# Weight groups of a quantised layer loaded ahead, page copies spread, and the inverses' row ahead of V, in a four-layer residual kernel

## The reference, cut to what matters

```python
x = x + L0(x)   # gated MLP (512 -> 1376 -> 512) with a LoRA adapter for each of the 8 sequences
x = x + L1(x)   # attention: 32 query heads, 8 key heads, 512 cached keys in pages + 128 new ones
x = x + L2(x)   # linear, weight quantised with a codebook and scale, plus a LoRA delta
x = x + L3(x)   # linear, one of 8 weights for each sequence

# L1, for each sequence and head
kc, vc = k_cache[block_table], v_cache[block_table]     # 16 pages of 32 keys
probs = softmax(where(valid, q @ k_all.T * SCALE, -1e30))
o = probs @ v_all ; y = o @ Wo.T

# L2: the weight is made once
wg = (weight + lora_delta).reshape(O, 4, 128) ; normalized = wg / exp(scale_log)
w_q = cb[searchsorted(thresholds, normalized)]          # passed through "+ normalized - normalized"
y = x @ (w_q * scale + lora_delta).T
```

## Time and profile before

| | us |
|---|---|
| median of three plain executions | 1434.79 |
| the profiled execution | 1438.17 |
| its span, first to last instruction | 1436.6 |
| TensorE busy (matmul) | 1378.2 |
| VectorE busy | 1020.5 |
| ScalarE busy | 980.1 |
| GpSimd busy | 748.7 |

### The profile page before, as it was taken

How to read it: one execution, slowest core, us unless ns; L and a number is a source line. 1 busy time by engine, 2 the same in 40 slices (tenths; PEclk the granted TensorE clock), 3 DMA queues, 4 the chain that set the end, 5 groups by cost and what they waited for, 6 DMA issues and landing times.

```text
span 1436.6 us, 26330 instructions
## 1 busy us (share of the span) xinstructions
PE 1378.2 (96%) x7812; PEld 1192.8 (83%) x7812; DVE 1020.5 (71%) x2111; ACT 980.1 (68%) x1986; POOL 748.7 (52%) x986
## 2 busy tenths in 40 slices
PE   7899897899999999999999999999999999999888
PEld 5788775688888888888888888888888888888766
DVE  4777666566777777777777777777777777777656
ACT  5666564467777687777776777777777777876643
POOL 5322222366666566656555665565566656655300
PEclk9999999999999999999999999999999999999989
DMA  8788778356332424333232334332323342322244
GB/s 196 229 263 274 229 182 270 99 135 174 96 89 60 104 59 113 71 98 77 72 104 60 90 73 115 63 89 60 103 60 95 75 111 60 89 59 60 40 173 147
DMA packets 256596, 165.80 MB, mean 115 GB/s; under 512 B 157398, under 2 KB 223575, under 8 KB 250951
## 3 DMA queue, kind: packets, MB, share of 16 engines
q1 hardware_dynamic: 250928, 144.51, 37.9%
q0 software_dynamic: 5376, 19.60, 4.8%
q10 hardware_dynamic: 150, 0.01, 0.0%
HBM read 158.66 MB, written 38.94 MB: 138 GB/s over the span
## 4 chain that ended last, share of the span: by engine, by line
PE 79%; DMA 5%; DVE 4%; ACT 3%; POOL 3%; issue 3%; SPq 2%; POOLq 0%; DVEq 0%; ACTq 0%
PE proj_ps L1366 16%; PE sc L1406 14%; PE o_ps L1444 13%; PE ring L1424 8%; PE sc L1161 5%; PE proj_ps L1460 4%; PE proj_ps L1463 4%; PE proj_ps L1471 4%; PE o_ps L1161 3%; DMA inv_row<-inv_dram 3%; PE proj_ps L1161 2%; DMA prep<-scale_dram 2%; PE ring L1483 2%; SPq L333 1%; POOL vl L631 1%
## 5 line engine op out<-in xcount | busy, mean ns | idle before, releaser
L1926 DVE TENSOR_TENSOR pTl<-ring,pTh 128x512 fp32r<-128x512 f32 x320 | 215.3, 690 | 144.7 <-ACT pTh L969 140.4
L958 ACT ACTIVATE p_sb<-p_sb,bias,rstd 128x640 f32<-128x640 f32 x256 | 236.0, 923 | 52.4 <-DVE bias L1909 52.4
L704 POOL TENSOR_TENSOR rstd<-var,half_neg 128x4 f32<-128x4 f32 x64 | 68.9, 1076 | 305.6 <-DVE var L1958 305.6
L1893 DVE CUSTOM_DVE_ANT_0 p_sb<-sc,mask 128x640 f32<-128x640 f32 x256 | 206.0, 823 | 23.7 <-PE sc L1406 17.9
L969 ACT ACTIVATE pTh<-ring 128x512 fp32r<-128x512 f32 x320 | 184.9, 601 | 27.7 <-PE ring L1424 26.4
L1424 PE MATMUL ring<-ident,p_sb 128*128 128x128 f32 x1280 | 181.4, 272 | 4.4 <-DVE pTl L1926 2.7
L1424 PEld LDWEIGHTS ring<-ident,p_sb 128*128 128x128 f32 x1280 | 152.8, 140 | 31.3 <-DVE pTl L1926 3.2
L1366 PE MATMUL proj_ps<-wh,xh 128*128 128x256 f32 (+1 forms) x484 | 168.2, 347 | 0.7 <-ACT q_sb L1005 0.7
L1406 PE MATMUL sc<-kTh,qTh 128*128 128x320 f32 x512 | 164.2, 321 | 2.9 <-DVE kTl L2000 2.9
L1366 PE MATMUL proj_ps<-wl,xh 128*128 128x256 f32 (+1 forms) x484 | 161.7, 334 | 0.0
L1005 ACT ACTIVATE q_sb<-proj_ps 128x512 f32<-128x512 f32 x64 | 38.3, 599 | 180.7 <-PE proj_ps L1366 172.2
(11 more groups left out here) (250 smaller groups left out, 3636.1 us busy)
## 6 DMA issues: line engine op xcount, KB each, us to landing
k_pages<-in_k_cache SPq DMA_DIRECT2D x128, 128.0 KB, 3.5
v_pages<-in_v_cache POOLq DMA_DIRECT2D x128, 128.0 KB, 3.7
k_raw<-k_pages SPq DMA_DIRECT2D x256, 64.0 KB, 2.6
v_raw<-v_pages SPq DMA_DIRECT2D x64, 256.0 KB, 3.0
rope<-rope_dram SPq DMA_DIRECT2D x64, 256.0 KB, 3.4
inv_row<-inv_dram SPq DMA_DIRECT2D x64, 256.0 KB, 3.9
stage<-in_Wqkv SPq DMA_DIRECT2D x32, 384.0 KB, 4.7
w_raw<-in_WguT SPq DMA_DIRECT2D x19, 512.0 KB, 4.8
```

The costliest lines, as they stand in the source:

```text
L704: pool.tensor_tensor(rstd[:, u.k % 2, 0:REP], var[:, u.k % 2, 0:REP], half_neg[:, 0:REP], ALU.pow).then_inc(S["q_pow"], 1)
L958: act_e.activation(p_sb[:, p_slot(u, h), :], p_sb[:, p_slot(u, h), :], ACT.Exp, bias=bias[:, h:h + 1], scale=rstd[:, u.k % 2, h:h + 1], ac ...
L1893: v.tensor_tensor_reduce(out=p_sb[:, p_slot(u, h), :].rearrange("p (s k) -> p s k", s=2), in0=score_ps[h % 2][:, :, 0:SPLIT], in1=mask[:, ...
L1926: v.tensor_tensor(pTl[:, c, :], ring[c % 2][:, :], pTh[:, c, :].bitcast(F32), ALU.subtract).then_inc(S["ptl"], 1)
```

## The change

Three parts. (1) Groups 1 to 3 of the quantised layer are loaded into `spare`, rows of the rotary table's tile, at q = 13, 16 and 20; `load_group` waits for the landing of the group before (group 1 also for the rotary table's write to DRAM, group 3 for group 2's stage 0) and no longer for its result. The results go to rows 2, 1, 0, 2 of `prep` (`made_row`); the wait for the store ahead of stage 0 goes, and group 3's result waits for the first store. The last group's stage 1 moves from right after `low_act(21)` to the step k = 2 of the last `down` steps, stage 2 from k = 3 to k = 4. (2) Key copies for each q come from a list, value copies are 4, then 3 (n = 11 to 15), then 7 (n = 16 to 21), then two for each block of W_down. Blocks of W_down 3 and 4 of the last steps are ordered ahead of the wait for `gate_up`; x is loaded at q = 18 and 21. (3) In a step of attention the row of inverses is ordered ahead of V, after two key copies where there are any. Some tiles of layers 1 and 2 are declared in another order.

```diff
+KEY_COPIES = [0] * 6 + [2, 2, 2, 3, 3] + [3] * 5 + [7] * 6
...
+        spare = rope_tab[:, :, :, :].rearrange("p k b d -> p (k b d)").rearrange("p (r n) -> p r n", n=HID)
...
+        def group_row(g, n):
+            return prep[:, n, :] if g == 0 else spare[:, 3 * (g % 2) + n, :]
+        def made_row(g):
+            return prep[:, (2, 1, 0, 2)[g], :]
...
                 else:
-                    sp.wait_ge(S["w2_ready"], g)
-                load(prep[:, 0, :], ins["W2T"][:, g, :], S["w2_in"])
...
+                    sp.wait_ge(S["w2_in"], 48 * g)
+                    if g == 1:
+                        sp.wait_ge(S["rope_in"], 16)
+                    if g == 3:
+                        sp.wait_ge(S["leaf_step"], 5)
+                load(group_row(g, 0), ins["W2T"][:, g, :], S["w2_in"])
...
-                sp.dma_start(w2_dram[:, g, :], prep[:, 4, :]).then_inc(S["put"], 16)
+                sp.dma_start(w2_dram[:, g, :], made_row(g)).then_inc(S["put"], 16)
...
-                if q == 13:
+                if q in (13, 16, 20):
+                    load_group({13: 1, 16: 2, 20: 3}[q])
+                if 19 <= q:
+                    load_wd(CH + q - 19)
+                if q == 18:
                     load(x_sb[:, 0:HALF, :], ins["x"][0:HALF].rearrange("b t n -> t b n"), x_in[0])
-                if q == 16:
+                if q == 21:
                     sp.wait_ge(S["xl_set"], 2 * C)
...
-                copy_keys(2 if q < FC else 5)
-                if q in (16, 19, 21):
+                if q in (16, 19):
                     store_group(q // 3 - 5)
-                    load_group(q // 3 - 4)
+                copy_keys(KEY_COPIES[q])
             copy_keys(5)
...
-            for n in range(FC):
-                if n >= 3:
-                    load_wd(CH + n)
-                    copy_keys(2)
-                if n == 5:
-                    store_group(3)
-                if n == 2:
+            store_group(2)
+            for n in range(3, FC):
+                load_wd(CH + n)
+                copy_keys(2)
+                if n == 4:
                     sp.wait_ge(S["gate_up"], 4 * FC)
                     for c in range(C):
                         load_wqkv(first, c)
                     load_k(first)
-                if n == 4:
+                if n == 5:
                     load_v(first)
...
+                if n == 6:
+                    store_group(3)
+                if n in (7, 9):
...
             def step(u):
                 put_inv(u + -2)
+                if u.k < B - 1:
+                    copy_keys(2)
+                spread_inv(u + -2)
                 if (u + -1).exists() and u.k > 1:
                     load_v(u + -1)
-                if 2 <= u.k < B - 1:
-                    copy_keys(2)
-                spread_inv(u + -2)
...
-                    copy_keys(6 if u.k < 2 else 4)
+                    copy_keys(4)
...
-                copy_values(4 if n < FC else 5)
-            pool.wait_ge(S["gate_up"], 4 * FC)
-            copy_values(18)
+                copy_values(4 if n < FC else 3 if n < 16 else 7)
+            for k in range(2, CH):
+                pool.wait_ge(S["wd_hi"], CH + k + 1)
+                copy_values(2)
...
-                if k == 5:
+                if k == 7:
                     act_e.wait_ge(S["put"], PUT_SCALES + 16 * C)
...
-                    if g:
-                        dve.wait_ge(S["put"], PUT_SCALES + 16 * g)
...
+                    if g == 3:
+                        dve.wait_ge(S["put"], PUT_SCALES + 16)
+                    v.tensor_tensor(made_row(g), tmp, delta, ALU.add).then_inc(S["w2_ready"], 1)
...
             low_act(2 * FC - 1)
-            weight2(*STAGES[2 * FC - 1])
...
                     low_t(1, 2)
-                if k == 3:
+                    weight2(*STAGES[2 * FC - 1])
+                if k == 4:
                     weight2(*STAGES[2 * FC])
```

More of the change, by code:

```diff
@@ L222, in cond_resid_kernel @@
         wl = l1_sb("wl", [P, C, QKV], F32R)
-        woh = l1_sb("woh", [P, REP, HID], F32R)
-        wol = l1_sb("wol", [P, REP, HID], F32R)
+        xh = l1_sb("xh", [P, B, C, T], F32R)
         rope = l1_sb("rope", [P, 2, 4, D])
@@ L227, in cond_resid_kernel @@
         v_raw = l1_sb("v_raw", [P, LC, D])
-        xh = l1_sb("xh", [P, B, C, T], F32R)
+        woh = l1_sb("woh", [P, REP, HID], F32R)
+        wol = l1_sb("wol", [P, REP, HID], F32R)
         xl = l1_sb("xl", [P, B, C, T], F32R)
@@ L269, in cond_resid_kernel @@
         w3_raw = l2_sb("w3_raw", [P, 2, C, HID])
+        w2_h = l2_sb("w2_h", [P, C, HID], F32R)
+        w2_l = l2_sb("w2_l", [P, C, HID], F32R)
         x2T_h = l2_sb("x2T_h", [P, 2, C * T], F32R)
@@ L274, in cond_resid_kernel @@
         w3_h = l2_sb("w3_h", [P, 2, C, HID], F32R)
-        w2_h = l2_sb("w2_h", [P, C, HID], F32R)
-        w2_l = l2_sb("w2_l", [P, C, HID], F32R)
         w3_l = l2_sb("w3_l", [P, 2, C, HID], F32R)
@@ L388, in load_group @@
                 else:
-                    sp.wait_ge(S["w2_ready"], g)
-                load(prep[:, 0, :], ins["W2T"][:, g, :], S["w2_in"])
-                load(prep[:, 1, :], scale_dram[0, g, :].partition_broadcast(P), S["w2_in"])
-                load(prep[:, 2, :], scale_dram[1, g, :].partition_broadcast(P), S["w2_in"])
+                    sp.wait_ge(S["w2_in"], 48 * g)
[4 more added lines that the diff above has]
+                load(group_row(g, 0), ins["W2T"][:, g, :], S["w2_in"])
+                load(group_row(g, 1), scale_dram[0, g, :].partition_broadcast(P), S["w2_in"])
+                load(group_row(g, 2), scale_dram[1, g, :].partition_broadcast(P), S["w2_in"])
             def store_group(g):
                 sp.wait_ge(S["w2_ready"], g + 1)
-                sp.dma_start(w2_dram[:, g, :], prep[:, 4, :]).then_inc(S["put"], 16)
+                sp.dma_start(w2_dram[:, g, :], made_row(g)).then_inc(S["put"], 16)
             load_x_chunk(0, 0)
@@ L423, in _ @@
                     load_wd(q - 8)
-                if q == 13:
+                if q in (13, 16, 20):
[3 more added lines that the diff above has]
+                if q == 18:
                     load(x_sb[:, 0:HALF, :], ins["x"][0:HALF].rearrange("b t n -> t b n"), x_in[0])
-                if q == 16:
+                if q == 21:
                     sp.wait_ge(S["xl_set"], 2 * C)
                     load(x_sb[:, HALF:, :], ins["x"][HALF:].rearrange("b t n -> t b n"), x_in[1])
-                if 19 <= q:
-                    load_wd(CH + q - 19)
-                copy_keys(2 if q < FC else 5)
-                if q in (16, 19, 21):
+                if q in (16, 19):
                     store_group(q // 3 - 5)
-                    load_group(q // 3 - 4)
+                copy_keys(KEY_COPIES[q])
             copy_keys(5)
@@ L490, in _ @@
                     load_rope(first)
-                if n in (6, 8):
-                    for h in (n - 6, n - 5):
+                if n == 6:
+                    store_group(3)
+                if n in (7, 9):
+                    for h in (n - 7, n - 6):
                         sp.wait_ge(S["wqkv_l"], h + 1)
@@ L1707, in weight2 @@
             def weight2(g, stage):
-                w, scale, norm, delta = (prep[:, n, :] for n in range(4))
+                w, scale, norm = (group_row(g, n) for n in range(3))
+                delta = prep[:, 3, :]
                 tmp = w
@@ L1731, in weight2 @@
                     then(v.tensor_tensor(tmp, tmp, scale, ALU.mult))
-                    v.tensor_tensor(leaf[0], tmp, delta, ALU.add).then_inc(S["w2_ready"], 1)
+                    if g == 3:
+                        dve.wait_ge(S["put"], PUT_SCALES + 16)
+                    v.tensor_tensor(made_row(g), tmp, delta, ALU.add).then_inc(S["w2_ready"], 1)
             def low_act(n):
```

## The result

The median of 11 plain executions is 1425.5 us (1420.3 to 1429.0), that of the kernel before on the same chip 1435.0 (11 executions, 1429.0 to 1437.4). The profiled executions stand at 1438.17 and 1428.24 us, 9.9 apart for a forecast of 19.6. The direction was right and the range (1411 to 1427) holds the median. But the sum was made from the profiled execution, and like with like, 1428.24 us, lies outside of it: some 40 to 50% of the gain is missing.

A forecast was written before the change was run, and what follows sets the result against it. TensorE was busy 96% of 1436.6 us, so gains had to come from its idle time or slow clock, some 58 us. Terms 10.3 + 0 + 2.5 + 6.8 = 19.6 took the profiled 1438.2 to 1418.6, range 1411 to 1427.

The forecast's parts named there:

- The groups' rows: Quantised layer, 104 to 230 us: earlier group loads remove TensorE's stalls and slow clock; 10.3 us, bounds 6 to 10.3.
- The copies up to block 21: SyncE's queue, q = 16 to 21: seven copies each stay within a margin of 1 to 5 us; cost 0, up to 3.5.
- Rival (c): SyncE's pacing: slower copies delay weight blocks, turning point 1.94 us spacing, 1447.6 us at 2.2; chance 0.04 full, 0.05 in part.
- The last `down` steps: 230 to 265 us: W_down blocks come less late, some 2.8 of 5.3 us idle stay; gain 2.5, bounds -1 to 5.3.
- the 2.6 of `lad_l`: The share of TensorE's 8.6 us of waits for `lad_l` forecast to go behind the end of `gate_up`; 2.6 us.
- a cost of 0: Price put on the new copy pacing, judged at weight block 21 on SyncE's queue; 0, upper bound 3.5 us.
- Stage 1 ahead of the fourth block: Last `down` steps: the last group's stage 1, 3.9 us, delays the fourth W_down block's split; a TensorE stall of 0.9 us.
- The loop's start: 265 to 300 us: a chain of latencies no edit touches; 0, with clock scatter worth 1.7 us either way.
- The row ahead of V: Attention loop: the row of inverses leaves sooner, ScalarE's waits shrink; 6.6 us plus 0.2, bounds 1 to 7.2 on the 6.6.
- (a): Weaker parts don't pay: last `down` steps give 0, the row of inverses 3; 1424.7 us; chance 0.30 together with (b).
- (b): Groups' stalls go but ScalarE takes over, so their part gives 6; 1422.9 us; chance 0.30 together with (a).
- (d): Gains don't add: TensorE's idle time moves to the loop's start; 1431 to 1436 us; chance 0.06.

The follow-up runs named there:

- e2: Changed kernel with V ordered ahead of the row of inverses again; 1428.0 us, ratio 0.9963.
- e11: Changed kernel with key and value copies paced as before the change, second run; 1419.4 us, ratio 0.9909.
- e8: Changed kernel with ten key copies for seven at each of q = 16 to 21; 1453.6 us in one execution.
- e10: Changed kernel run again with no edit; 1425.6 us, ratio 0.9956.
- e6: Changed kernel with the same transfers reordered on SyncE's queue, blocks of W_down at their earliest; 1416.9 us, ratio 0.9887.
- e9: Changed kernel with the order of e6 and the last group's stage 1 in three pieces; 1414.7 us, ratio 0.9885.
- e4: Changed kernel with the last group's stage 1 back right after the last `low_act`; 1425.7 us, ratio 0.9951.
- e12: Kernel before the change, run again with no edit for a second profile; 1433.7 us in one execution.
- e3: Changed kernel with key and value copies paced as before the change, first run; 1420.4 us, ratio 0.9909.
- e1: Kernel before with only the row of inverses ordered ahead of V; 1428.3 us, ratio 0.9967.
- e5: Changed kernel with the page copies beside the last W_down blocks moved into the loop's first steps; 1426.6 us, ratio 0.9942.

## Why the prediction was right or wrong

**The groups' rows: right.** -8.3 us up to G for -7.7. VectorE's wait for `prep<-scale_dram` is gone, so are the waits for `lad_l` and the half clock of the earlier trace rows; TensorE itself is what is late next, with 0.5 us idle in 108.4. G was forecast near 213 and came at 212.4. e2 to e11 repeat it (106.7 to 111.2 us for 116.3 to 116.7), e8 apart.

**The copies up to block 21: right.** Block 21 was forecast to be issued at 191 us and was at 192.6, with no wait of TensorE behind it; ScalarE waited 4.9 us for that block, which the slack covered. Rival (c) asked for slower orders, 1.94 us apart, and none came (1.25 to 1.39); e8 shows the same harm from more orders at the same spacing, and bounds the margin: block 21 ordered 22.4 us later brought 13.9 us more of idle time before G (14.4 for 0.5), so an estimate of it from these two runs is some 8 us, where the prediction had 1 to 5.

**The last `down` steps: the step that failed.** The prediction gave them -2.5 us, besides the 2.6 of `lad_l`; they got longer by 1.5, and so were 6.6 us over the forecast: 5.4 in idle time (8.5 for 3.1), 1.7 at half clock, and 0.5 of busy time the other way. Two terms of the step were wrong; both are about SyncE's queue. First, "a cost of 0" for the copies was taken at block 21 only. SyncE's lateness was inside the margin there and I let it drop, but the queue goes on: twelve copies (14.71 us) stand between block 21 and the next block of W_down, which goes out at 210.66 us, where the old pace has it at 204.10 (e11). With the order as it is, the new spread costs about 6 us, by e10 and e11; by e6 this lateness costs nothing that shows once the order is mended, so the two are not separate losses to be added. Second, the gain was put down to the two blocks ordered ahead of Wqkv and to the burst of value copies taken away. But block 6 still stands behind Wqkv's four loads and the keys' four and goes at 222.03, block 7 behind V, rotary rows and copies at 230.06. Where "blocks 7 and 8 still come 0 to 1.5 us late", the run has 2.0 us before block 7, 0.35 before block 8 and 3.1 before block 9, which had not been counted at all. e6 settles that it is the queue: the same transfers, reordered, give 38.9 us, which is the 39.2 that the prediction had for this stage, with the stage before it 1.7 us shorter as well. The bounds of this term, -1 to 5.3, did not hold it: it is a loss of 4.1 (1.5 more, and the 2.6 of `lad_l` used up). They took in neither the queue's lateness nor the clock; only with the up to 3.5 us that the prediction allowed for the copies at block 21 do they reach it. The sum's size was wrong in this term, and the kinds of wait were named.

**Stage 1 ahead of the fourth block.** Counted as a stall of 0.9 us from 222.6 on; it was 1.99, up to 223.93, and a half clock of 3.4 us stood behind it, 1.7 more. e9 shows what it is worth once the blocks come in time (37.6 us for the 38.9 of e6). e4 shows that it can't be had by putting the stage back.

**The loop's start: 0 forecast, +1.9.** Idle time is the same (10.0 for 9.7), the half clock 13.7 for 10.2 us, which is 1.75. Two profiles of one kernel differ by as much and more: 10.2 and 13.7 us (the first profile before and e12), 13.7 and 6.8 (e3 and e11), at 9.7 to 10.0 us idle. So this looks like scatter between executions, about the "1.7 us either way" of the prediction; no effect of the change is shown.

**The row ahead of V: right mechanism, size off by three.** 6.8 us forecast, 5.2 in the loop by the profiled pair, of which 3.3 are the event at units 21 to 23 that e12 doesn't have (loops of 1030.9 and 1027.6 us). The profiled pair owes a third of its whole gain of 9.9 us to that event, which is luck and not the change. The prediction had named this possibility, but left the 2.1 + 1.7 us in its sum. What stays is 1.9: by e12, 0.6 in units 1 to 5 (84.4 for 83.8) and some 1.2 at the heads' changes. A change takes 17.28 us after and 17.28 to 17.83 before, the event apart, so 0 to 0.5 us each for 0.35. ScalarE's 15.5 us of waits went to 0, and 6.1 us for `q_cos` came instead, the successor that the prediction named. The plain executions of e1 say 4.7 us (2.7 to 6.6); whether the rest over 1.9 is seldom-met waits like that of unit 22, which one profile can't show, stays open. Over 64 units the row goes 1.40 to 3.41 us after the inverses, half of them within 1.43; the prediction had 1.4 to 2.8.

**The median.** Against the medians the forecast was 1419.0 and the time 1425.5, 6.5 off, and 1.5 inside the range's edge. That it fell inside owes something to luck: the sum started from a profiled execution 3.4 us over the median; from the median the same 19.6 us give 1415.2, 10.3 off. e11, the same kernel with the old copies, has 1419.4, but not by the forecast's terms: its last `down` steps take 41.0 us for 39.2.

**The rivals.** (a), weaker parts that don't pay, named the right parts at 1424.7 us, of which the down steps were to give 0 and the row 3; they cost 4.1, and the row gave 5.2 in the profiled pair, of which 1.9 stay. Its 1424.7 is the nearest to the median, but it is made from the slower profiled execution too; against 1428.24 it is 3.5 short. (b) didn't come: 0.5 us for ScalarE. (d) did in part: what TensorE gained before G stayed, what it gained behind G went; its price (1431 to 1436) didn't come.

## What to carry to other kernels

When a queue of orders falls behind within its margin, carry the lateness on to the next consumer on that queue rather than dropping it where the first one is safe: here it was harmless at block 21 and, with the order of the queue as it was, cost some 6 us twenty microseconds later. Before moving traffic away from a late load, look at what is ordered ahead of it on the same queue; here the same transfers in another order gave some 8 us (ratio 0.9887 for 0.9941), while moving the copies to the loop gave nothing in all. And an event that one profiled execution shows once goes into the sum only when a second profile has it too.

## What the runs showed of the hardware

An order for a block of W_down right behind eight loads took SyncE 3.87 us to issue (2.97 in e10, 3.33 in e11, and 3.35 in e5 without any page copy beside it), 1.59 behind four loads (e6), and 0.41 to 0.62 for the other blocks of that stage in the kernel after: an order can cost its queue some seven times the usual. Page copies of 128 KB were issued 1.29 us apart with twelve in a row (14.71 less 0.5, over eleven) and 1.30 with ten (e8). In rows of five before it was 1.25 to 1.50, and in rows of seven after 1.25 to 1.39, at a DMA share of 0.81 over the stage: the cost of one such order did not rise with their number. The half clock behind a like idle time (9.6 to 10.0 us, D to O0) lasted 6.8, 10.2 or 13.7 us in different executions, which alone is 3.4 us of scatter from one profile to the next and as much as the smaller parts of this change.
